# A two-product graph layer on one core: handling the column panels in pairs

## The reference

```python
h = max(layernorm(x), 0)
u = par_u[0] * par_u[1] * (diag_u[:, None] * h[:2048] @ W_u) + h[:2048]
i = par_i[0] * par_i[1] * (diag_i[:, None] * h[2048:] @ W_i) + h[2048:]
e = concatenate([u, i])                   # 5120 x 64
y = adj @ (adj.T @ e)                     # the two large products
out = x + (y - mean) * rsqrt(var + 1e-5) * gamma + beta + h
```

## Time and profile before

| | |
|---|---|
| median of 3 runs | 401.11 us (399.4 to 401.13) |
| the profiled execution | 400.56 us, of which 398.4 us are the span in the trace |
| TensorE matmul busy | 376.8 us, 95% of the span |
| VectorE busy | 294.2 us, 74% |
| ScalarE, GpSimd busy | 31.0 us, 19.9 us |
| moved by DMA | 128.88 MB, mean 323 GB/s |
| mean granted clock of TensorE | 0.983 |

### The profile page before, as it was taken

One profiled execution on the slowest core, in us unless ns is written; L12 is line 12 of the kernel. 1 busy time (PEld: TensorE's weight loads), 2 busy tenths in 40 slices (PEclk: granted clock), 3 DMA queues, 4 the chain that ended last, 5 costly groups with the idle time before them and its releaser, 6 DMA issues.

```text
span 398.4 us, 9972 instructions
## 1 busy us (share of the span) xinstructions
PE 376.8 (95%) x4484; PEld 192.8 (48%) x4484; DVE 294.2 (74%) x320; ACT 31.0 (8%) x90; POOL 19.9 (5%) x26
## 2 busy tenths in 40 slices
PE   6778699999999999999999999999999999999991
PEld 2445336455554645455463545545354554536451
DVE  5488799795966859595785959577595958759347
ACT  4343200000000000000000000000000000000032
POOL 1121700000000000000000000000000000000013
PEclk9699989999999999999999999999999999999998
DMA  8999779989797978979797897979798797950003
GB/s 312 422 421 419 297 259 390 369 334 400 315 424 308 426 298 352 388 313 424 304 428 299 370 365 311 425 309 426 302 388 349 312 425 302 424 192 2 3 0 132
DMA packets 18878, 128.88 MB, mean 323 GB/s; under 512 B 2096, under 2 KB 2224, under 8 KB 3504
## 3 DMA queue, kind: packets, MB, share of 16 engines
q1 hardware_dynamic: 18288, 127.63, 79.2%
q10 hardware_dynamic: 576, 1.05, 0.7%
HBM read 127.36 MB, written 1.31 MB: 323 GB/s over the span
## 4 chain that ended last, share of the span: by engine, by line
PE 88%; DVE 6%; ACT 3%; issue 2%; DMA 1%; DVEq 0%
PE t_acc L464 43%; PE h_acc L493 35%; PE h_acc L477 9%; ACT h_in L259 2%; DVE var L330 1%; DMA xs<-x 1%; DVE centred L377 1%; DVE scaled L428 1%; DVE e L354 1%; DVE scaled L424 1%; PE h_acc L442 1%; DVE centred L325 0%; DVE total L319 0%; PE t_acc L521 0%; DVE xs L431 0%
## 5 line engine op out<-in xcount | busy, mean ns | idle before, releaser
L362 DVE STREAM_TRANSPOSE strips<-natural 128x2048 f32<-128x2048 f32 x80 | 178.0, 2281 | 69.0 <-PE h_acc L493 69.0
L464 PE MATMUL t_acc<-natural,e 128*64 128x256 f32 x1600 | 181.9, 385 | 5.6 <-DVE e L354 5.6
L464 PEld LDWEIGHTS t_acc<-natural,e 128*64 128x64 f32 x1600 | 113.1, 138 | 77.7 <-issue 17.0
L493 PE MATMUL h_acc<-strips,centred 32*64 32x512 f32 x2560 | 142.6, 592 | 0.0
L493 PEld LDWEIGHTS h_acc<-strips,centred 32*64 32x64 f32 x2560 | 54.6, 132 | 87.1 <-issue 87.1
L377 DVE STREAM_TRANSPOSE centred<-t_sum 32x256 f32<-32x256 f32 x160 | 69.6, 435 | 2.6
L477 PE MATMUL h_acc<-cols,centred 128*64 128x512 f32 x160 | 39.1, 611 | 3.2 <-DVE centred L377 3.2
L274 ACT COPY t_high<-t_acc 64x256 f32<-64x256 f32 x20 | 7.4, 368 | 318.6 <-PE t_acc L464 318.6
L230 POOL TENSOR_TENSOR xs<-scaled,xs 128x512 f32<-128x512 f32 x4 | 5.1, 1269 | 339.1 <-DVE scaled L428 339.1
L477 PEld LDWEIGHTS h_acc<-cols,centred 128*64 128x64 f32 x160 | 11.5, 138 | 18.6 <-issue 16.0
L372 DVE TENSOR_TENSOR t_sum<-t_acc,t_high 64x512 f32<-64x512 f32 x20 | 13.6, 680 | 3.6 <-ACT t_high L274 3.5
(11 more groups left out here) (37 smaller groups left out, 50.0 us busy)
## 6 DMA issues: line engine op xcount, KB each, us to landing
natural<-adj_rows SPq DMA_DIRECT2D x100, 1024.0 KB, 10.9
cols<-adj_cols SPq DMA_DIRECT2D x20, 1024.0 KB, 4.8
out<-xs SPq DMA_DIRECT2D x5, 256.0 KB, 2.0
xs<-x ACTq DMA_DIRECT2D x4, 256.0 KB, 6.1
xs<-x SPq DMA_DIRECT2D x1, 256.0 KB, 3.6
smalls<-small SPq DMA_DIRECT2D x1, 214.0 KB, 4.3
```

The lines of the kernel that those rows point to most:

```text
L362: nc.vector.transpose(strips[:, a, :, m].rearrange("p c t i -> p t c i"), natural[:, a, m].rearrange("p t (c j) -> p t c j", j=Q)).then_in ...
L464: last = nc.tensor.matmul(t_acc[D * s:D * (s + 1), a, 0:WIDE], e[:, GT * m + HALF * s + k, :], natural[:, a, m, HALF * s + k], start=(m == ...
L493: last = nc.tensor.matmul(h_acc[D * s:D * (s + 1), q], t[part, a, b, u, :], rows, start=(isinstance(g, int) and g == 0 and b == 0 and u == 0),
```

## The change

Panels go in pairs. TensorE's `pair(g)` is product 1 of g and of g+1, the loaded part of g, the row-tiled parts of g and g+1, and the loaded part of g+1. The lag of one panel between the products is gone within a pair, and the loop covers all pairs from 2 to 17. VectorE's `pair` is the eight turns of both panels and then both `keep_t`; `keep_t` of an odd panel has a new wait on `s_loaded_done`, since the loaded part of the odd panel before now comes last and still reads that buffer. SyncE's loads of `cols` move: `cols` of an even panel stands behind the `natural` loads of the odd panel after it, and `cols` of an odd panel stands ahead of the `natural` loads of the next even panel. ScalarE's work keeps its order. GpSimd is not touched. The number of instructions of each kind stays the same. Behind the work on the input, TensorE now does the loaded part of panel 0, the row-tiled parts of 0 and 1, and the loaded part of 1, before product 1 of panel 2.

```diff
-        def middle_steps(eng, step):
+        def pairs(eng, pair):
             with eng.Fori(1, PANELS // 2 - 1) as i:
-                step(2 * i, 0, i)
-                step(2 * i + 1, 1, i)
-            step(LAST - 1, 0, LAST // 2)
+                pair(2 * i, i)
+            pair(LAST - 1, LAST // 2)
...
             for g in range(2, PANELS):
+                if g % 2 == 0 and g > 2:
+                    sp.wait_ge(s_loaded_done, g - 2)
+                    load_cols(g - 1)
                 for m in range(GROUPS):
...
                     load_natural(g, m)
-                sp.wait_ge(s_loaded_done, g - 1)
-                load_cols(g)
+                if g % 2:
+                    sp.wait_ge(s_loaded_done, g - 2)
+                    load_cols(g - 1)
+            sp.wait_ge(s_loaded_done, LAST - 1)
+            load_cols(LAST)
...
-            def step(g, a, half):
-                keep_t_high(g, a, firsts(g, GROUPS - 1))
+            def pair(g, half):
+                keep_t_high(g, 0, firsts(g, GROUPS - 1))
+                keep_t_high(g + 1, 1, firsts(g + 1, GROUPS - 1))
...
                 dve.wait_ge(s_t_sum, g + 1)
+                if a == 1 and not (isinstance(g, int) and g < 2):
+                    dve.wait_ge(s_loaded_done, g - 1)
...
-            def step(g, a, half):
-                for m in range(TURNED):
-                    turn_strips(g, a, half, m)
-                keep_t(g, a)
+            def pair(g, half):
+                for a in range(2):
+                    for m in range(TURNED):
+                        turn_strips(g + a, a, half, m)
+                for a in range(2):
+                    keep_t(g + a, a)
...
-            def step(g, a, half):
-                for m in range(GROUPS):
-                    first(g, a, half, m)
-                second_loaded(g - 1, 1 - a, half - 1 + a)
-                second_strips(g - 1, 1 - a).then_inc(s_strips_done, 1)
+            def both_first(g, half):
+                for a in range(2):
+                    for m in range(GROUPS):
+                        first(g + a, a, half, m)
+
+            def pair(g, half):
+                both_first(g, half)
+                second_loaded(g, 0, half)
+                for a in range(2):
+                    second_strips(g + a, a).then_inc(s_strips_done, 1)
+                second_loaded(g + 1, 1, half)
...
             second_loaded(0, 0, 0)
-            second_strips(0, 0).then_inc(s_strips_done, 1)
-            middle_steps(pe, step)
-            for m in range(GROUPS):
-                first(LAST, LAST % 2, LAST // 2, m)
+            for a in range(2):
+                second_strips(a, a).then_inc(s_strips_done, 1)
+            second_loaded(1, 1, 0)
+            with pe.Fori(1, PANELS // 2 - 1) as i:
+                pair(2 * i, i)
+            both_first(LAST - 1, LAST // 2)
             second_strips(LAST - 1, 0).then_inc(s_strips_done, 1)
             second_strips(LAST, 1).then_inc(s_strips_last, 1)
```

## The result

The changed kernel has a median of 402.86 us (402.78 to 403.68, 5 runs), the kernel before 400.97 us beside it (399.12 to 401.13). The ratio is 1.0067, 95% interval 1.0039 to 1.0094. Forecast were 402.6 us within 400.0 to 404.0. The profiled execution of after has 402.83 us and a span of 400.6 us, against 400.56 and 398.4 before.

The account below looks back on a forecast made before the run. TensorE's own sequence was taken to bound the kernel. On the profiled 400.56 us, +2.9 for the stall and -2.5 for seams, as walked +0.3, and +1.7 for the clock gave 402.6 us, range 400.0 to 404.0.

Parts of the forecast that it names:

- What bounds the kernel: From panel 2 on, TensorE's own sequence bounds, 17.55 us a panel; loads, at 14.7 us, are close behind.
- The gap at the start: Before the row-tiled part of panel 1, TensorE stands idle for 2.90 us, waiting for VectorE's turns.
- The walk from the turns: At panel 1, the fourth turn ends at 62.88, so its row-tiled part starts at 63.03.
- The fall of the clock behind it: Behind the 2.90 us gap at panel 1, the clock falls to half, costing 1.7 us; the other end is 0.
- The seams: TensorE's excursions into 32-row matmuls drop from 19 to 10, gaining 9 x 0.28 = 2.5 us (1.6 at the lower end).
- The sum: Whole kernel: stall +2.9, seams -2.5, as walked +0.3, and clock +1.7 on 400.56 us give 402.6 us.
- rival 2: In the pairs, VectorE becomes the bound if turns exceed their 3.7 us slack; about 410 us, chance 0.05.
- rival 1: Behind the new gap at panel 1 the clock holds, so without the 1.7 us: 400.9 us, chance 0.30.
- rival 3: Seams cost more, or the half clock at 50.4 to 53.7 goes as well: faster, 399.2 us for the latter; chance 0.07.
- rival 4: At the seams the change gives nothing, the loss moving to other seams: 405.2 us, chance 0.05.
- the 1.9 us of the earlier trace: TensorE idle about 1.9 us at 29.1 to 31.0, clock staying at 1.00 for 15 us behind it; spoke for no fall.

Follow-up runs that it names:

- the filled gap: Changed kernel with ten matmuls, results unused, between the row-tiled parts of panels 0 and 1, the wait for the turns kept: 399.56 us, 1.78 below the changed kernel.
- The seams added to the kernel before: Kernel before with the loaded part moved between the two halves of the row-tiled part in the steps for panels 2 to 18: 406.34 us, ratio 1.0167.
- the second profile of the same kernel: The changed kernel run again unchanged, beside the kernel before: 401.34 us, ratio 1.0040.
- The kernel with two turns more: Changed kernel with two VectorE turns done twice in each pair from panel 2 on: 408.84 us, ratio 1.0234 to the kernel before.
- one more turn: Changed kernel with one VectorE turn done twice in each pair from panel 2 on: 402.94 us, ratio 1.0053 to the kernel before.
- less filling: Changed kernel with six matmuls instead of ten between the row-tiled parts of panels 0 and 1: 401.08 us, ratio 1.0033 to the kernel before.

## Why the prediction was right, step by step

- **What bounds the kernel.** Right: no wait for loads or for t appears in the pairs, though SyncE's order was changed, and the only new wait of TensorE is the one named.
- **The gap at the start.** Forecast 2.90 us. The row-tiled part of panel 0 lasts until 53.81 + 7.00 = 60.81 and that of panel 1 starts at 63.58: 2.77 us. The walk from the turns was right: it put the start of the part of panel 1 at 63.03 - 49.71 = 13.32 us behind the loaded part of panel 0, and it lies 13.23 behind.
- **The fall of the clock behind it.** Forecast 1.68 us, the one term that rested on a choice between two rows. Measured 1.76 us in the profile, or 1.70 against the 7.06 us that the same part takes in the filled gap, and 1.78 us between medians when the gap was filled. The size and the sign were right. The reason given for the choice, that 2.90 us are nearer to the wait that was followed by a fall than to the one that wasn't, does not hold: in the same trace of before the clock fell in a wait of 1.76 us (last section). So that the fall came as forecast is in part luck.
- **The seams.** Mis-sized: forecast 9 x 0.28 = 2.5 us, with "no room for more". A pair is 34.77, not 34.82, so an excursion is worth (35.10 - 34.77) = 0.33 us, 9 x 0.33 = 3.0. The failed step took the 8.68 us of product 1 as free of loss. Behind the loaded part two of them take 74.11 to 91.37 = 17.26 us, 8.63 each; behind row tiles there were 0.05 us more inside it. The seams added to the kernel before gave 0.34.
- **The sum.** From the loaded part of panel 0 on: 2.77 + 1.76 - 3.0 = 1.5 us, measured 1.54; forecast 2.0. The missing half microsecond was made up by 0.64 us that the sum didn't have: in the profile of after, TensorE reached that point at 50.35 instead of 49.71, with two stretches of half clock in its work on the input instead of one. In the second profile of the same kernel it was 48.87, with one. So 402.6 lies near 402.86 partly by luck; on the other chip the same kernel was 0.4% slower.
- **VectorE's slack** (rival 2). Forecast 3.7 us; in the second pair of after the t of panel 4 is ready at 122.42 and used at 126.14, 3.7 us. The kernel with two turns more passes the point at which it decides, by 0.9 us a pair from start to start.
- **The clock holds** (rival 1). Not in either profile of after. It may hold in part of the executions: the fastest, 399.38 us at a mean clock of 0.984, has less half clock than the 0.981 of the traced one. But that could also be a stretch in the input work, so it is not shown.
- **The first fall goes** (rival 3). This rival took 1.7 us off the changed kernel for it. The runs show that it saves nothing there: VectorE sets when panel 1 starts, and the gap grows by as much (last section). It saves time only in the kernel before.
- **Nothing gained at the seams** (rival 4). Ruled out by the pair of 34.77 us and by the seams added to the kernel before.

## What to carry to other kernels

A regrouping that saves seams has to be priced where the pipeline fills as well: here 3.0 us over the whole run were outweighed by 4.5 us at its one entry, because the work that used to hide a neighbour engine's preparation had moved behind its use. Keep the first step in the old order and start the new one a step later. And where TensorE must wait near the start, give it matmuls that are wanted later: filling removes the idle time and the half clock behind it.

## What the runs showed of the hardware

The length of an idle stretch alone did not decide whether the clock fell. The stretch of 3.16 or 3.17 us ahead of the loaded part of panel 0 stands in ten traces. It was followed by half clock in seven, among them before and after, and not in those of the added seams, of one more turn and of less filling. The stretch of 2.6 to 2.8 us ahead of the row-tiled part of panel 1 was followed by it four times, and once not (2.79 us, less filling). And in the trace of before the clock fell in a wait of 1.76 us, from 11.84 to 13.60, in the input work (granted clock third from the end), where TensorE had also been idle for 1.72 and 0.89 us shortly before:

```profile
11.90:12.70 0.80, 0.00 (x0) 0.00 (x0) 0.80 (x1) 0.00 (x0) 0.49 (x1) 1.00 1.07 451
12.70:13.50 0.80, 0.00 (x0) 0.00 (x0) 0.80 (x3) 0.53 (x1) 0.00 (x0) 0.50 0.93 389
```

So the 1.9 us of the earlier trace rows, behind which the clock held, are not a safe length. The Trainium skill, TensorE: Matmul & The Clock Gate, on the HAM clock gate, says that half rate is what idle brings back; the filled gap agrees. The ten traces show that the same work up to that point may or may not meet it.

In the changed kernel the first fall costs nothing. VectorE sets when the row-tiled part of panel 1 starts: 13.23 us behind the loaded part of panel 0 in after (63.58 - 50.35), and the same 13.23 with one more turn and with less filling (61.49 - 48.26), where the first fall is absent. With one more turn the gap is larger for it:

```profile
50.80 1.94 PE L490 MATMUL h_acc<-cols,centred 128*64 128x512 f32 x8 [3.16 <-DVE centred L389]
52.67 7.12 PE L506 MATMUL h_acc<-strips,centred 32*64 32x512 f32 x128
64.03 9.93 PE L506 MATMUL h_acc<-strips,centred 32*64 32x512 f32 x128 [4.24 <-DVE strips L372]
```

There the part of panel 1 lasts until 73.89, 9.86 us: half clock lasted for most of it (0.52 on the mean from 64.1 to 70.0 us). That is 2.8 us over the 7.06 of the filled gap, where the fall in after costs 1.7.
